# Two row products and a softmax sum ahead of a chain of small steps, and a move's wait split in two

## The chip, the cores and the metric

One Trainium2 chip, one core of it. The metric is the device time of one execution in microseconds (us), lower is better. Names of engines: PE is TensorE, DVE is VectorE, ACT is ScalarE, POOL is GpSimd, SP is SyncE. Each runs its own instructions in program order; between engines a semaphore wait decides.

## The reference

Four stages run one after the other on x of shape (16, 256, 128): a linear attention, a mixture of experts, a feature-map attention and a deep stage of six layers. Only the deep stage is touched. Its attention, for each of 16 sequences of 256 tokens and in each of six layers:

```python
qkv = x @ Wqkv                         # 128 -> 3 * 1024, 16 heads of 64
q = l2norm(q) * qs ; k = l2norm(k) * ksc
q = q * cos * scale + rotate_half(q) * sin * scale
k = k * cos * inv   + rotate_half(k) * sin * inv
sim = einsum(q, k over the own and the previous window of 32) * 8.0, masked
attn = softmax(sim, -1)
out = einsum(attn, v) ; x = out @ Wo + x
```

and then a feed-forward layer with a layer norm and an exact gelu, over blocks of two sequences. All in float32; the projections are split into a high and a low part.

## The kernel before, in words

The deep stage (`deep_stage`) is a software pipeline over 96 sequences (6 layers of 16), taken in pairs. A pair is a frame of 32 steps, 16 for its even and 16 for its odd sequence. In each step every engine runs, in this order: the late part of the attention of the sequence before, the early part of the attention of this one, the projection work of the sequence two ahead, the projection work of the sequence one ahead, and the feed-forward block's part. Tables of step numbers (`TOTAL_STEPS`, `NORM_STEPS`, `SCALE_STEPS`, `NEWTON_STEP` and others) say at which step a piece of work is issued; a step of 16 or more is one that falls into the next sequence's frame, and a negative one into that of the sequence two ahead or one ahead. The order on each engine is thus written out, and the engines wait for each other by semaphores.

Names and lines that matter here. For every sequence:

- DVE, L1900 `ss`: sums of squares of q and k per head, four reductions. L1919 to L1934, `inverse`: twelve dependent instructions on 128x64 numbers, the inverse square root by a bit trick and three Newton steps, result `rs`. They are issued at step 14 of a sequence for the sequence two ahead.
- DVE, L1906 and L1913: the rotary cosine product of a 128x1024 part of `raw`, and the addition of the sine part, which lies in `spare`. Four of each (k is the half of the tokens, part 0 is q, part 1 is k). Both read two tensors in SBUF.
- POOL, L2129: the sine products into `spare`, four. L2137: `raw` times `rs`, the scaling of q and k, four; the first of them is issued at step 14 and waits for `rs`. L2154: the softmax's product `E` times `rden`, two instructions of 128x512 for each group of eight heads.
- DVE, L1964 and L1970: row maximum of the scores and the subtraction, reading PSUM. ACT L1817: exp. DVE, L1977 and L1979, `totals`: row sum of `E` and its reciprocal `rden`.
- PE, L1654: transposes of `E`; L1565 to L1567: the projections, and the feed-forward's gate and up products; L1640: scores; L1672: attention times v.
- DVE, L2019 `xnT_lo`: low part of the feed-forward's input, at step 14 of the even sequence; PE's gate products (L1565) need it. L2027 `hT`: DVE's product of gate and up. L1941 and L1943 `xT_lo`: low part of the next projection's input. L2003 to L2012: the layer norm's statistics, in the frames' odd halves.
- SP, L1466 to L1469, `move_v`: sixteen DMAs that lay v out for the windows (`Vw`), after ACT has drained v's four parts from PSUM (L1801, `v_drained`). They are followed in SP's queue by the loads of `xs` and `xs4`.

The heads come in two groups of eight, o = 0 and o = 1. Group 1's sum, product and so on have the second number of each table.

Of the kernel before, what the change touches and what calls it, by code (L numbers as in the profile page):

```python
# [40 lines left out]
def count(n):  # L41


    return n + 1
# [1107 lines left out]
VS = 4  # L1152
# [19 lines left out]
SCORE_STEPS = (0, 5)  # L1172
HIGHEST_STEPS = (4, 10)
EXP_STEPS = (5, 12)
TOTAL_STEPS = (9, 15)
NORM_STEPS = (8, 16)
FLIP_STEPS = (11, 18)
MIX_STEPS = (13, 21)
DRAIN_STEPS = (15, 22)
# [108 lines left out]
def deep_stage(nc, X, c, w, kept, raw, split, wqkv_hi, wqkv_lo, out, x_out):  # L1288
    with ExitStack() as ctx:
# [5 lines left out]
        def sem(name):  # L1295
            counters.append(ctx.enter_context(nc.semaphore(name)))
            return counters[-1]
# [81 lines left out]
        v_drained = sem("v_drained")  # L1379
# [49 lines left out]
        def _(sp):  # L1429
# [28 lines left out]

            def move_v(n, par):

                sp.wait_ge(v_drained, count(VS * n + VS))
                for hp in range(2):
                    v = V[:, :, hp * 512:hp * 512 + 512]
                    own, back = 64 * hp + WIN, 64 * hp
                    for g in range(4):
                        sp.dma_start(Vw[own:own + WIN, par, :, g], v[g * WIN:g * WIN + WIN]).then_inc(v_moved[par], 16)  # L1466
                    for g in range(1, 4):
                        sp.dma_start(Vw[back:back + WIN, par, :, g], v[g * WIN - WIN:g * WIN]).then_inc(v_moved[par], 16)
                    sp.dma_start(Vw[back:back + WIN, par, 1, 0], v[P - WIN:P, 0]).then_inc(v_moved[par], 16)  # L1469
# [23 lines left out]
            def body(q):  # L1493
                if q.has(3):
                    bring(q, 3)
                if q.at(7) and q.has(2):
                    load_table(q.l + 1, 2)
                    load_table(q.l + 1, 3)
                if q.has(1):
                    move_v(q.n + 1, 1)  # L1500
                if q.opens(0) and q.has(0) and q.has(-1):
                    load_wo(q.l)
                if q.has_block(-1):
                    shift_block(q)
                if q.has(4):
                    bring(q, 4)
                if q.at(6) and q.has(4):
                    load_table(q.l + 1, 0)
                    load_table(q.l + 1, 1)
                if q.has(2):  # L1510
                    move_v(q.n + 2, 0)
# [6 lines left out]
            load_ffn(0)  # L1518
            bring(Pair(0, 0), 2)
            move_v(0, 0)  # L1520
            body(Pair(0, 0))
            body(Pair(0, 1))
# [370 lines left out]
        def _(dve):  # L1893
# [66 lines left out]
            def highest(n, o):  # L1960
                N = 2 * n + o
                dve.wait_ge(scored, count(N + 1))
                s = sco[:].rearrange("p b (c j) -> p (b c) j", j=HD)
                dve.tensor_reduce(mx[:], s, AX.X, ALU.max).then_inc(maxed, 1)  # L1964
                dve.wait_ge(maxed, count(N + 1))
                if not (isinstance(N, int) and N < 2):
                    dve.wait_ge(p_turned, count(2 * N - 2))
                s = sco[:].rearrange("p h (s j) -> p h s j", j=HD)
                m = mx[:].rearrange("p (h s) -> p h s", h=2)
                dve.tensor_tensor(E[:, o].rearrange("p (s h) j -> p h s j", h=2), s,  # L1970
                                  m[:, :, :, None].to_broadcast([P, 2, ROWS // 2, HD]),
                                  ALU.subtract).then_inc(lowered, 1)

            def totals(n, o):
                N = 2 * n + o
                dve.wait_ge(exped, count(N + 1))
                dve.tensor_reduce(den[:, o], E[:, o], AX.X, ALU.add).then_inc(totalled, 1)  # L1977
                dve.wait_ge(totalled, count(N + 1))
                dve.reciprocal(rden[:, o], den[:, o]).then_inc(recips, 1)  # L1979
# [7 lines left out]
            def attend(q, d, step):  # L1987

                for o in range(2):
                    if step == HIGHEST_STEPS[o]:  # L1990
                        highest(q.n + d, o)
                    if step == TOTAL_STEPS[o]:
                        totals(q.n + d, o)
# [123 lines left out]
        def _(pool):  # L2117
# [29 lines left out]
            def attend(n, step):  # L2147
                for o in range(2):
                    if step == NORM_STEPS[o]:
                        N = 2 * n + o  # L2150
# [196 lines left out]
```

## Time and profile before

| | |
|---|---|
| median of 3 runs | 4786.8 us (4783.35 to 4789.63) |
| the profiled execution | 4788.12 us, span 4786.4 us |
| DVE busy | 4071.3 us (85%) |
| PE busy | 4232.6 us (88%), matmul ends modelled |
| ACT busy | 3053.7 us (64%) |
| POOL busy | 3012.7 us (63%) |

The deep stage takes the stretch from about 1300 us to the end. It is periodic: a pair of sequences takes some 70 us. Busy time contains stretched time: an instruction that had to wait for something within itself is shown longer, not later. Idle time of an engine is shown ahead of the instruction that ended it, with the releaser.

### The profile page before, as it was taken

Reading aid. Unit: us, or ns where it says so; the run is one execution under the profiler, and the core shown is the slowest. Engines: PE = TensorE matmul, PEld = TensorE weight load, DVE = VectorE, ACT = ScalarE, POOL = GpSimd, SP = SyncE. Lnnn points to the kernel's source line nnn. Section 1 sums busy time; section 2 is a strip of 40 time slices with the busy share of each in tenths; the row PEclk is TensorE's granted clock in tenths of the full one; section 3 lists DMA queues with packets and bytes.
Section 4 is the critical chain, followed back from the end, with each engine's and each line's share of the span. In section 5 each row is a group of like instructions: output and inputs, shape, how many; then the busy total and the mean of one; then the engine's idle time right before and its main releaser. Section 6 shows DMA issues by size and latency. Waiting matters only on the chain.

```text
span 4786.4 us, 164817 instructions
## 1 busy us (share of the span) xinstructions
PE 4232.6 (88%) x70208; PEld 3350.3 (70%) x70208; DVE 4071.3 (85%) x6282; ACT 3053.7 (64%) x5515; POOL 3012.7 (63%) x1586
## 2 busy tenths in 40 slices
PE   5698699999668999999999998999989999999996
PEld 4566377877656777777777777777767777777775
DVE  4344699999788999999989999899998999989995
ACT  3365333333156777777777777777777777777773
POOL 0222566666267767677776777767776677766772
PEclk9699799999889999999999999999999999999998
DMA  1234000000023234232332323333242332433322
GB/s 50 78 127 141 0 1 0 0 0 0 19 54 76 58 70 95 63 81 62 75 88 64 84 58 90 80 67 75 60 101 66 67 77 58 96 74 67 75 58 74
DMA packets 237661, 302.78 MB, mean 63 GB/s; under 512 B 92500, under 2 KB 127832, under 8 KB 236504
## 3 DMA queue, kind: packets, MB, share of 16 engines
q1 hardware_dynamic: 221752, 247.08, 22.7%
q0 software_dynamic: 15264, 46.14, 3.1%
q8 instruction: 522, 8.55, 0.8%
q14 instruction: 123, 1.01, 0.1%
HBM read 50.37 MB, written 28.84 MB: 17 GB/s over the span
## 4 chain that ended last, share of the span: by engine, by line
DVE 41%; PE 14%; issue 9%; POOL 5%; ACT 4%; SPq 1%; DMA 0%; POOLq 0%; DVEq 0%; ACTq 0%
DVE raw L1906 10%; DVE raw L1913 8%; DVE mx L1964 3%; DVE E L1970 3%; DVE ss L1900 3%; PE shared L1565 2%; PE acc L1672 2%; DVE den L1977 2%; PE sco L1640 2%; POOL spare L2129 2%; POOL raw L2137 2%; DVE hT L2027 2%; PE shared L1567 2%; PE shared L1566 1%; ACT raw L1783 1%
## 5 line engine op out<-in xcount | busy, mean ns | idle before, releaser
L2137 POOL TENSOR_TENSOR raw<-raw,rs 128x1024 f32<-128x1024 f32 x384 | 794.4, 2069 | 887.4 <-DVE rs L1934 551.8
L2129 POOL TENSOR_TENSOR spare<-raw,table 128x1024 f32<-128x1024 f32 x384 | 969.7, 2536 | 79.1 <-DVE raw L1913 63.3
L1906 DVE TENSOR_TENSOR raw<-raw,table 128x1024 f32<-128x1024 f32 x384 | 667.9, 1739 | 87.1 <-POOL spare L2129 85.5
L1913 DVE TENSOR_TENSOR raw<-raw,spare 128x1024 f32<-128x1024 f32 x384 | 725.5, 1889 | 13.2
L1783 ACT ACTIVATE raw<-shared 128x512 f32<-128x512 f32 x768 | 463.2, 603 | 311.2 <-PE shared L1567 280.2
L1565 PE MATMUL shared<-wqkv_lo,xT_hi 128*128 128x512 f32 x1152 | 550.0, 477 | 57.1 <-DVE xT_lo L1943 49.0
L2154 POOL TENSOR_TENSOR E<-E,rden 128x512 f32<-128x512 f32 x384 | 544.2, 1438 | 30.8 <-DVE rden L1979 30.8
L1900 DVE TENSOR_REDUCE ss<-spare 128x16 f32<-128x1024 f32 x384 | 463.8, 1208 | 62.3 <-ACT spare L1788 61.9
L1620 PE MATMUL trn<-ident,raw 128*128 128x128 f32 x3072 | 485.2, 281 | 6.9 <-POOL raw L2137 3.4
L1567 PE MATMUL shared<-wqkv_hi,xT_hi 128*128 128x512 f32 x1152 | 462.6, 402 | 0.0
L1566 PE MATMUL shared<-wqkv_hi,xT_lo 128*128 128x512 f32 x1152 | 462.2, 401 | 0.0
L1788 ACT ACTIVATE spare<-shared 128x512 f32<-128x512 f32 x768 | 461.2, 601 | 1.3 <-DVE ss L1900 1.3
L1620 PEld LDWEIGHTS trn<-ident,raw 128*128 128x128 f32 x3072 | 352.6, 141 | 132.7 <-ACT qT L1810 76.5
L1672 PE MATMUL acc<-prT,Vw 64*64 64x32 f32 x24576 | 440.4, 221 | 2.2 <-issue 2.2
L1821 ACT ACTIVATE prT<-trn 128x512 f32<-128x512 f32 x384 | 232.0, 604 | 303.8 <-PE trn L1654 303.5
L1672 PEld LDWEIGHTS acc<-prT,Vw 64*64 64x64 f32 x24576 | 397.6, 136 | 25.3 <-issue 2.4
L1688 PE MATMUL shared<-wo,oT 128*128 128x128 f32 x3072 | 376.1, 276 | 2.3 <-ACT oT L1830 1.3
L1688 PEld LDWEIGHTS shared<-wo,oT 128*128 128x128 f32 x3072 | 363.4, 193 | 8.6 <-ACT spare L1788 1.5
L1640 PE MATMUL sco<-kT,qT 64*32 64x64 f32 (+1 forms) x24576 | 354.8, 223 | 12.5 <-issue 12.2
L1640 PEld LDWEIGHTS sco<-kT,qT 64*32 64x32 f32 x24576 | 240.9, 108 | 169.7 <-issue 165.4
L1654 PE MATMUL trn<-ident,E 128*128 128x128 f32 x1536 | 250.1, 287 | 112.9 <-POOL E L2154 109.1
L1565 PEld LDWEIGHTS shared<-wqkv_lo,xT_hi 128*128 128x128 f32 x1152 | 221.7, 192 | 133.7 <-issue 43.0
(208 smaller groups left out, 9678.4 us busy)
## 6 DMA issues: line engine op xcount, KB each, us to landing
Vw<-V SPq DMA_DIRECT2D x1344, 128.0 KB
xs<-X SPq DMA_DIRECT2D x144, 128.0 KB, 2.6
Vw<-V SPq DMA_DIRECT2D x192, 64.0 KB
e_plain<-in_L_ffn_W SPq DMA_DIRECT2D x16, 704.0 KB, 4.6
split_hi<-e_high POOLq DMA_DIRECT2D x16, 704.0 KB, 5.9
split_lo<-e_low POOLq DMA_DIRECT2D x16, 704.0 KB, 7.0
wqkv_hi<-split_hi POOLq DMA_DIRECT2D x30, 256.0 KB, 3.1
wqkv_lo<-split_lo POOLq DMA_DIRECT2D x30, 256.0 KB, 3.2
```

The lines of the kernel that those rows point to most:

```text
L1565: pe.matmul(to, a_hi, b_lo, start=True, stop=False)
L1567: return pe.matmul(to, a_hi, b_hi, start=False, stop=True)
L1620: t = pe.transpose(trn[:, r * P:(r + 1) * P], raw[:, par, k, part, at:at + P], c["ident"][:])
L1640: t = pe.matmul(sco[g * WIN:g * WIN + WIN, hp, at:at + back + WIN], qT[lo:lo + 64, r, at_q:at_q + WIN], kT[lo:lo + 64, r, at_q - back:at_q ...
L1672: t = pe.matmul(acc[hp][64 * jp:64 * jp + 64, at:at + WIN], Vw[lo:lo + 64, par, k, g, (4 * o + j) * HD:(4 * o + j + 1) * HD], prT[lo:lo + ...
L1688: t = pe.matmul(to[:, k * P:(k + 1) * P], oT[:, r, k * P:(k + 1) * P], wo[:, r], start=(r == 0), stop=(r == PAIRS - 1))
L1900: dve.tensor_reduce(ss[:, j * H:(j + 1) * H], heads_of(sq[:, part]), AX.X, ALU.add).then_inc(reduced, 1)
L1906: dve.tensor_tensor(x, x, table[:, part, 0, k][:, None, :].to_broadcast([P, H, HD]), ALU.mult).then_inc(cos_part, 1)
L1913: dve.tensor_tensor(x, x, t2[:, part], ALU.add).then_inc(summed, 1)
L2129: pool.tensor_tensor(dst, src, by[:, None].to_broadcast([P, H, 2, 32]), ALU.mult).then_inc(sin_part, 1)
L2137: pool.tensor_tensor(x, x, rs[:, at:at + H][:, :, None].to_broadcast([P, H, HD]), ALU.mult).then_inc(rotated, 1)
L2154: pool.tensor_tensor(E[:, o, rows], E[:, o, rows], rden[:, o, rows][:, :, None].to_broadcast([P, ROWS // 2, HD]), ALU.mult).then_inc(norme ...
```

## The change

Three edits, all in the deep stage.

1. DVE's `totals` for the second eight heads moves from step 15 to step 14. Within step 14 the attention part comes first, so it now stands ahead of the twelve instructions of `inverse`.
2. POOL's product `E` times `rden` for the second eight heads moves from step 16 to step 14. It now stands ahead of the first scaling of q.
3. `move_v` waited once for all four parts of v; now it waits for two parts ahead of its first eight DMAs, and for all four ahead of its second eight.

```diff
-TOTAL_STEPS = (9, 15)
-NORM_STEPS = (8, 16)
+TOTAL_STEPS = (9, 14)
+NORM_STEPS = (8, 14)
...
             def move_v(n, par):
 
-                sp.wait_ge(v_drained, count(VS * n + VS))
                 for hp in range(2):
+                    sp.wait_ge(v_drained, count(VS * n + 2 * hp + 2))
                     v = V[:, :, hp * 512:hp * 512 + 512]
```

On DVE, around the end of an odd sequence, before the change (`na` and `rs` are Newton's, `den` and `rden` the sum and its reciprocal, `xT_lo` the next projection's input):

```order
 L1931 SCALAR_TENSOR_TENSOR na<-na,rs 128x64
 L1934 SCALAR_TENSOR_TENSOR rs<-na,rs 128x64
 L1977 TENSOR_REDUCE den<-E 128x16
 L1979 RECIPROCAL rden<-den 128x16
 L1941 TENSOR_TENSOR xT_lo<-shared,xT_hi 64x256
```

and the same place after it, from the last reduction of the squares:

```order
 L1900 TENSOR_REDUCE ss<-spare 128x16
 L1977 TENSOR_REDUCE den<-E 128x16
 L1979 RECIPROCAL rden<-den 128x16
 L1919 TENSOR_SCALAR hx<-ss 128x64
 L1921 TENSOR_SCALAR na<-hx 128x64
 L1925 TENSOR_TENSOR rs<-magic,na 128x64
```

The sum and the reciprocal moved from behind the twelve instructions to before them.

On DVE at the end of an even sequence, where the feed-forward's `xnT_lo` and `hT` stand, before:

```order
 L1934 SCALAR_TENSOR_TENSOR rs<-na,rs 128x64
 L2019 TENSOR_TENSOR xnT_lo<-hT,xnT_hi 128x512
 L1977 TENSOR_REDUCE den<-E 128x16
 L1979 RECIPROCAL rden<-den 128x16
 L1941 TENSOR_TENSOR xT_lo<-shared,xT_hi 64x256
 L1943 TENSOR_TENSOR xT_lo<-shared,xT_hi 64x256
 L2027 SCALAR_TENSOR_TENSOR hT<-shared,b,hT 128x512
```

and after:

```order
 L1934 SCALAR_TENSOR_TENSOR rs<-na,rs 128x64
 L2019 TENSOR_TENSOR xnT_lo<-hT,xnT_hi 128x512
 L1941 TENSOR_TENSOR xT_lo<-shared,xT_hi 64x256
 L1943 TENSOR_TENSOR xT_lo<-shared,xT_hi 64x256
 L2027 SCALAR_TENSOR_TENSOR hT<-shared,b,hT 128x512
```

Between `xnT_lo` and `hT` the sum and the reciprocal are gone.

On POOL, one sequence, before (the first `raw` row is the first scaling of q, `E` the second eight heads' product, `spare` the sine products):

```order
 L2129 TENSOR_TENSOR spare<-raw,table 128x1024
 L2137 TENSOR_TENSOR raw<-raw,rs 128x1024
 L2154 TENSOR_TENSOR E<-E,rden 128x512 x2
 L2137 TENSOR_TENSOR raw<-raw,rs 128x1024 x2
 L2129 TENSOR_TENSOR spare<-raw,table 128x1024
```

and after:

```order
 L2129 TENSOR_TENSOR spare<-raw,table 128x1024
 L2154 TENSOR_TENSOR E<-E,rden 128x512 x2
 L2137 TENSOR_TENSOR raw<-raw,rs 128x1024 x3
 L2129 TENSOR_TENSOR spare<-raw,table 128x1024
```

The two instructions on `E` moved ahead of the first scaling, and the three scalings now follow one another.

## Rows read from the trace of the kernel before

**Rows 1.** Busy time by engine in a stretch (us, PE, PEld, DVE, ACT, POOL, clock, DMA)
```profile
2000.00:3000.00 1000.00, 921.79 (x18923) 730.60 (x18923) 932.49 (x1230) 759.77 (x1328) 729.72 (x383) 0.99 0.34 75
```
**Rows 2.** Part 4 of the page, the chain that ended last, by engine
```profile
DVE 41%; PE 14%; issue 9%; POOL 5%; ACT 4%; SPq 1%; DMA 0%; POOLq 0%; DVEq 0%; ACTq 0%
```
**Rows 3.** Groups by line, DVE, 1400 to 4700 us (busy us, mean ns, idle)
```profile
L1913 DVE TENSOR_TENSOR raw<-raw,spare 128x1024 f32<-128x1024 f32 x374 | 703.2, 1880 | 12.8
L1906 DVE TENSOR_TENSOR raw<-raw,table 128x1024 f32<-128x1024 f32 x374 | 650.2, 1739 | 80.8 <-POOL spare L2129 79.3
```
**Rows 4.** Timeline of DVE, end of an even sequence (start us, us)
```profile
2240.86 0.19 DVE L1919 TENSOR_SCALAR hx<-ss 128x64 f32<-128x64 f32 x1
2241.09 0.20 DVE L1921 TENSOR_SCALAR na<-hx 128x64 int32<-128x64 int32 x1
...
2243.66 0.22 DVE L1934 SCALAR_TENSOR_TENSOR rs<-na,rs 128x64 f32<-128x64 f32 x1
2243.80 0.68 DVE L2019 TENSOR_TENSOR xnT_lo<-hT,xnT_hi 128x512 fp32r<-128x512 f32 x1
2244.40 1.21 DVE L1977 TENSOR_REDUCE den<-E 128x16 f32<-128x1024 f32 x1
2245.65 0.25 DVE L1979 RECIPROCAL rden<-den 128x16 f32<-128x16 f32 x1
2245.82 0.35 DVE L1941 TENSOR_TENSOR xT_lo<-shared,xT_hi 64x256 fp32r<-64x256 f32 x1
...
2246.65 0.75 DVE L2027 SCALAR_TENSOR_TENSOR hT<-shared,b,hT 128x512 f32<-128x512 f32 x1
2247.32 2.02 DVE L1906 TENSOR_TENSOR raw<-raw,table 128x1024 f32<-128x1024 f32 x1
2249.36 2.81 DVE L1913 TENSOR_TENSOR raw<-raw,spare 128x1024 f32<-128x1024 f32 x1
2252.10 1.21 DVE L1964 TENSOR_REDUCE mx<-sco 128x16 f32<-128x1024 f32 x1
```
**Rows 5.** Timeline of POOL, an odd and an even sequence's end
```profile
2211.41 2.04 POOL L2154 TENSOR_TENSOR E<-E,rden 128x512 f32<-128x512 f32 x2
2213.41 1.91 POOL L2137 TENSOR_TENSOR raw<-raw,rs 128x1024 f32<-128x1024 f32 x1
2215.27 1.99 POOL L2184 TENSOR_TENSOR small<-small,halves 128x4 f32<-128x4 f32 x1
...
2243.96 2.29 POOL L2137 TENSOR_TENSOR raw<-raw,rs 128x1024 f32<-128x1024 f32 x1 [5.35 <-DVE rs L1934]
2246.21 2.04 POOL L2154 TENSOR_TENSOR E<-E,rden 128x512 f32<-128x512 f32 x2
2248.21 2.88 POOL L2137 TENSOR_TENSOR raw<-raw,rs 128x1024 f32<-128x1024 f32 x1
```
**Rows 6.** Timeline of DVE, end of an odd sequence
```profile
2206.45 0.20 DVE L1919 TENSOR_SCALAR hx<-ss 128x64 f32<-128x64 f32 x1
...
2209.24 0.23 DVE L1934 SCALAR_TENSOR_TENSOR rs<-na,rs 128x64 f32<-128x64 f32 x1
...
2212.76 0.72 DVE L2012 TENSOR_SCALAR small<-mv 128x4 f32<-128x4 f32 x1
...
2214.28 2.12 DVE L1906 TENSOR_TENSOR raw<-raw,table 128x1024 f32<-128x1024 f32 x1
...
2217.69 1.23 DVE L1964 TENSOR_REDUCE mx<-sco 128x16 f32<-128x1024 f32 x1
```
**Rows 7.** Timeline of DVE, late, the same L2012 with POOL idle
```profile
4757.30 0.17 DVE L2012 TENSOR_SCALAR small<-mv 128x4 f32<-128x4 f32 x1
```
**Rows 8.** Waits, 1000 to 4700 us (us in total, times, longest)
```profile
POOL raw L2137 <- DVE rs L1934: 551.8, 96, 6.6
PE trn L1654 <- POOL E L2154: 109.1, 91, 4.1
DVE mx L1964 <- PE sco L1640: 16.4, 7, 3.8
```
**Rows 9.** Timeline of ACT, the exp ahead of the odd sum
```profile
2204.63 1.06 ACT L1817 ACTIVATE E<-E 128x1024 f32<-128x1024 f32 x1
```
**Rows 10.** Waits of SP's own queue, 1500 to 4650 us
```profile
SPq L1466 <- ACT V L1801: 1756.4, 90, 27.5
```

## The prediction, made before the changed kernel ran

> **What bounds the kernel.** I read the busy times by stretch first. In the deep stage PE and DVE are both busy over 92% of the time, ACT and POOL some 75% [rows 1]. The chain that ended last is mostly DVE, 41% of the whole span against PE's 14% [rows 2]. The reader should then look at how long DVE's two largest groups take. L1906 and L1913 average 1.74 and 1.88 us [rows 3], though the sum over a 128x1024 tile takes 1.21 us [rows 4], and single ones of these two take 1.2 us when POOL does nothing. So a good part of "busy" DVE is waiting inside its instructions.
>
> The timelines of DVE and POOL side by side show for what. L1906 starts at 2247.32, lasts 2.02 and ends at 2249.34; POOL's two products on E end at 2248.25 [rows 4, 5], about 1.1 us before that. POOL's next scaling, started at 2248.21, takes 2.88 us instead of 1.91, and L1913 behind L1906 takes 2.81 and ends at 2252.17, 1.1 us after that scaling. The two engines take turns, one instruction at a time: whoever comes second waits for the whole instruction of the other. It is no matter of size: the layer norm's 4-element L2012 takes 0.72 us beside POOL's product on E and ends with it (2213.48 against 2213.45) [rows 5, 6], and 0.17 us with POOL idle [rows 7]. Sums over a tile (L1977, L1964) stay at 1.21 to 1.23 us whatever POOL does.
>
> That row decides this case, because the twelve Newton instructions now run alone. POOL is idle through them in every one of the 96 sequences, waiting for their result [rows 8], so each takes 0.19 to 0.23 us and they follow at 0.26 us: 2240.86 to 2243.88, 3.02 us [rows 4]. The change starts the two E products just when they begin.
>
> **The change part by part.** Time 0 below is where Newton starts before. I follow the DVE until it starts the maximum of the next scores (L1964), which before is at 11.24 in the even sequence (2252.10) and at 11.24 in the odd one (2217.69) [rows 4, 6]. From there the engines' order is as before.
>
> *The sum and its reciprocal ahead.* Work is only exchanged: 1.42 us (2244.40 to 2245.82) [rows 4] go before Newton instead of behind. Newton starts at 1.42, and without any disturbance ends at 4.44.
>
> *E ahead of the first scaling.* The reciprocal ends at 1.50; POOL starts what it waited for 0.08 us after its releaser (2243.88 to 2243.96), so at 1.58. Each of the two products takes 1.02 us [rows 5]. Newton's first instruction is through by then. The second is ready at 1.65 and waits for the first product, to 2.6: 0.95 lost. It takes a turn, the second product follows (2.7 to 3.7), and the third instruction waits 0.85. Behind that POOL has nothing that could run, the scaling needs `rs`. So Newton is stretched by 1.8 us and ends at 6.25 instead of 3.02. The trace has no Newton instruction beside POOL; the bounds of this term are 0 (if instructions this small are not held, as those that sum are not) and 2.06 (both products whole). I take 1.8, by the L2012 row, which is as small and is held.
>
> The Trainium skill ("SBUF — State Buffer", section "SBUF: two separate sides") says that VectorE and GpSimd share a pair of ports as an exclusive lock, taken by VectorE instructions with two SBUF inputs or in a two-port mode, and that "the other fully blocks". It speaks against this change, as ten of the twelve have two SBUF inputs. By that rule the stretch is the 1.8 us taken here; the trace agrees with 0.72 against 0.17 us.
>
> *Even sequence, behind Newton.* POOL: first scaling from 6.33; beside `xnT_lo` it takes 2.25 to the next start, the second scaling 1.86, so POOL is occupied to 10.44 [rows 5]. DVE: `xnT_lo` 0.60. Then PE's gate products, gelu and `hT`: before, `hT` started 2.17 us after `xnT_lo` ended (2244.48 to 2246.65), and the sum and `xT_lo` covered that exactly. The sum's 1.42 are gone from there, only `xT_lo`'s 0.8 is left, so DVE now idles up to 1.35 us and starts `hT` at about 9.0. After its 0.67 L1906 is asked for at 9.7, in the middle of the second scaling, and waits to 10.44 (this wait would be there without the idle time too, so the idle time costs nothing of its own here). L1906 1.21 and L1913 1.23, which now meets no POOL instruction, bring L1964 to 12.85: 1.6 us later. What was gained is inside: L1906 and L1913 were held 2.4 us together, now 0.75.
>
> *Odd sequence.* POOL's two scalings follow from 6.33 at 1.86 each, to 10.1. DVE reached L1906 4.81 us behind Newton (2209.47 to 2214.28) [rows 6]; take off 1.42 for the sum and 0.5 for L2012, which meets the change of two scalings and waits little: asked at 9.15, held to 10.1. With L1906 and L1913 L1964 starts at 12.55, 1.3 us later. POOL's power instruction (1.99, L2184) falls beside L1913 as before and does not hold it.
>
> *What PE gets.* E is ready some 3 us earlier, and PE's wait for it, 109.1 us in 91 cases [rows 8], mostly goes. But DVE waited for scores only 7 times, 16.4 us in all [rows 8]: PE stood ahead of DVE at that place, so this is worth at most 16 us. And in the even sequence PE gets `xnT_lo` 3.2 us later, its gates end 3.2 us later, so its own wait for E is replaced by that one.
>
> *The moves of v.* The first eight DMAs start two drains earlier. SP's queue is idle 1756.4 us over 90 such waits [rows 10], nobody is shown waiting for `Vw` or for room in V. Behind the new second wait stand eight DMAs and the loads of `xs`, `xs4`, which go out no later than before since the count is the same. I cost it at 0; if the cover of some 20 us per sequence were gone it would show as a PE wait.
>
> **The sum.** (1.6 + 1.3) / 2 = 1.45 us over 96 sequences: 139 us. Chunk-loading frames and the 16 us of PE are of either sign and are left inside the range. The profiled execution took 4788.1 us, so 4927; the median of the runs lies 1.3 below it: 4926. The delay sits on the chain of waits, as DVE is on it without a gap from the second eight heads' maximum through Newton to L1964 of the next sequence, and the PE and ACT work behind starts from L1970.
>
> **Rivals.**
> - *Newton is not held* (faster). Ends at 4.44; L1906 starts when the scalings end, at 8.63 and 8.24, and L1964 at 11.05 and 10.7: 0.2 and 0.55 us earlier, 36 us in all, 4751. For it: no row shows a 64-element two-input instruction held, and the reductions aren't. Against: L2012. It decides at a stretch of 0.35 us: below that the change gains.
> - *Held once.* The two products run without a gap and Newton's second and third share one wait, or POOL starts late. Stretch 0.95, L1964 at 12.0 and 11.7: 0.6 us per sequence, 4844. Against: after each of its products POOL let DVE in (L1906 was let in between E and the scaling).
> - *A new wait decides as well.* The exp of the second heads ends at 2205.69 [rows 9], 0.76 us before Newton begins in the odd sequence; the sum now stands right there and Newton no longer covers it. Where ACT is late this adds up to 0.5 us per odd sequence, and PE, 2 us late in the even one, some 0.35 more: 41 us on top, 4967.
> - *Nothing moves the end*, PE being the bound and DVE's extra hidden: within 10 us of 4787. Against: L1964 waits for PE seven times in 96.
>
> **Chances.** Forecast 0.67, held once 0.12, new wait as well 0.06, not held 0.11, nothing 0.04. A time can be told from no change by about 0.2%, 10 us. So slower 0.85, same 0.04, faster 0.11. The range, 4825 to 4970, holds the forecast, the one with the new wait and most of held once; it leaves out the not-held case.
>
> **What would show it.** Right: the second and third Newton instruction (L1921, L1925, or one of the next) at about 1 us each, sum of L1919 to L1934 up by some 170 us over 96 sequences; L1906 and L1913 down by some 100 us; POOL's wait for `rs` still there, shorter by E's 2.1 but longer by the stretch; DVE idle ahead of `hT` up to 1.35 us in even sequences; PE's wait for E nearly gone, its wait for `xnT_lo` longer; no wait on `Vw`. Wrong: Newton's instructions still at 0.2 us with POOL's E products beside them.

## The result, and the profile after

The changed kernel takes 4925.8 us (median of 4 runs, 4922.16 to 4931.44), the kernel before beside it 4788.2: a ratio of 1.029, 95% interval 1.0277 to 1.0303. The change costs 138 us. The forecast was 4926; its total is right, and its working is right in part only.

Part 1 of the page after: DVE has lost busy share, not gained it.

```profile
PE 4297.2 (87%) x70208; PEld 3418.1 (69%) x70208; DVE 4049.1 (82%) x6282; ACT 3050.5 (62%) x5515; POOL 2862.8 (58%) x1586
```

The chain that ended last, which was DVE 41% and PE 14% [rows 2]:

```profile
PE 46%; DVE 15%; issue 7%; ACT 4%; POOL 1%; DMA 0%; POOLq 0%; DVEq 0%; SPq 0%
```

The groups of DVE by line, 1400 to 4800 us (busy us, mean ns | idle), against [rows 3] and the two lines of the kernel before that follow:

```profile
L1906 DVE TENSOR_TENSOR raw<-raw,table 128x1024 f32<-128x1024 f32 x371 | 646.8, 1743 | 62.4 <-POOL spare L2129 60.5
L1913 DVE TENSOR_TENSOR raw<-raw,spare 128x1024 f32<-128x1024 f32 x371 | 540.5, 1457 | 12.7
L1900 DVE TENSOR_REDUCE ss<-spare 128x16 f32<-128x1024 f32 x372 | 451.5, 1214 | 128.4 <-ACT spare L1788 128.4
...
L1929 DVE TENSOR_TENSOR na<-rs,hx 128x64 f32<-128x64 f32 x279 | 132.1, 473 | 9.6
L1925 DVE TENSOR_TENSOR rs<-magic,na 128x64 int32<-128x64 int32 x93 | 86.0, 925 | 5.4 <-DVE na L1921 2.6
```

```profile
L1900 DVE TENSOR_REDUCE ss<-spare 128x16 f32<-128x1024 f32 x373 | 450.6, 1208 | 56.7 <-ACT spare L1788 56.3
...
L2027 DVE SCALAR_TENSOR_TENSOR hT<-shared,b,hT 128x512 f32<-128x512 f32 x144 | 107.1, 744 | 17.8 <-ACT hT L1859 10.9 <-PE shared L1567 5.7
```

Two of Newton's twelve are held: L1925 takes 0.925 us, and L1929, which comes three times per sequence, averages 0.473. Against 0.225 each that is 0.70 + 3 x 0.25 = 1.44 us per sequence. L1913 meets fewer of POOL's instructions, 1.46 us instead of 1.88; L1906 is as before.

So the hold as such does not show up in DVE's busy time. It is 139 us over the 96 sequences, and L1913 gives back 159. What grows is DVE's idle time: ahead of `hT` from 17.8 to 95.2 us, and ahead of the sums of squares (L1900), which wait for ACT, from 56.7 to 128.4. The loss appears as waits for PE and ACT.

The end of one even sequence on DVE and on POOL (start us, us), to be read beside [rows 4, 5]:

```profile
2202.28 1.21 DVE L1900 TENSOR_REDUCE ss<-spare 128x16 f32<-128x1024 f32 x1
2203.41 1.21 DVE L1977 TENSOR_REDUCE den<-E 128x16 f32<-128x1024 f32 x1
...
2204.99 0.20 DVE L1921 TENSOR_SCALAR na<-hx 128x64 int32<-128x64 int32 x1
2205.22 0.95 DVE L1925 TENSOR_TENSOR rs<-magic,na 128x64 int32<-128x64 int32 x1
2206.20 0.97 DVE L1929 TENSOR_TENSOR na<-rs,hx 128x64 f32<-128x64 f32 x1
...
2209.16 0.69 DVE L2019 TENSOR_TENSOR xnT_lo<-hT,xnT_hi 128x512 fp32r<-128x512 f32 x1
...
2212.95 0.75 DVE L2027 SCALAR_TENSOR_TENSOR hT<-shared,b,hT 128x512 f32<-128x512 f32 x1 [2.33 <-PE shared L1567]
2213.62 1.22 DVE L1906 TENSOR_TENSOR raw<-raw,table 128x1024 f32<-128x1024 f32 x1
...
2216.62 1.23 DVE L1964 TENSOR_REDUCE mx<-sco 128x16 f32<-128x1024 f32 x1 [0.53 <-PE sco L1640]
```

```profile
2204.98 2.10 POOL L2154 TENSOR_TENSOR E<-E,rden 128x512 f32<-128x512 f32 x2 [4.96 <-DVE rden L1979]
2209.32 4.14 POOL L2137 TENSOR_TENSOR raw<-raw,rs 128x1024 f32<-128x1024 f32 x2 [2.24 <-DVE rs L1934]
```

POOL's two products run 2204.98 to 2207.08, and the two held instructions end with the first of them and with the second (2206.17, 2207.17). Newton's 3.02 us became 4.42 (2204.82 to about 2209.24). Then the part that the forecast priced at nothing: DVE idles 2.33 us ahead of `hT`. PE had waited since the end of its transposes for `xnT_lo`, and when it starts, its granted clock is the lower one. PE's timeline and the granted clock of the stretch:

```profile
2209.95 0.77 PE L1565 MATMUL shared<-xnT_lo,w_hi 128*128 128x512 f32 x1 [3.87 <-issue]
2210.51 0.63 PE L1566 MATMUL shared<-xnT_hi,w_lo 128*128 128x512 f32 x1
```

```profile
2209.90:2213.00 3.10, 3.05 (x8) 2.40 (x9) 0.75 (x3) 0.69 (x1) 3.10 (x2) 0.50 0.73 163
2213.00:2216.00 3.00, 3.00 (x43) 2.10 (x41) 2.97 (x3) 0.87 (x2) 0.47 (x1) 0.61 0.41 87
2216.00:2222.00 6.00, 6.00 (x150) 4.54 (x149) 5.10 (x6) 5.83 (x11) 4.26 (x2) 1.00 0.08 25
```

The column before the last two is the clock: 0.50, the lower of TensorE's two levels (1.2 GHz), behind an idle time of 3.87 us, and back at 1.00 after some 6 us. The products start 0.43 us apart instead of 0.23.

The waits after, 1000 to 4850 us (us in total, times, longest):

```profile
POOL raw L2137 <- DVE rs L1934: 221.2, 96, 5.3
PE shared L1565 <- issue: 191.0, 50, 4.4
...
PE shared L1565 <- DVE xT_lo L1943: 114.6, 46, 12.3
DVE hT L2027 <- PE shared L1567: 95.2, 45, 2.3
...
DVE mx L1964 <- PE sco L1640: 19.5, 25, 3.2
DVE den L1977 <- ACT E L1817: 18.1, 32, 3.0
```

The first two waits of PE in the kernel before, in the same stretch:

```profile
PE shared L1565 <- issue: 60.6, 50, 1.7
...
PE shared L1565 <- DVE xT_lo L1943: 49.0, 37, 12.3
```

PE's wait for E (109.1 us) [rows 8] is down to 4.2 us in 3 cases, and two others grew: the one ahead of the gates, whose input is `xnT_lo`, from 60.6 to 191.0 us, and the one for `xT_lo` from 49.0 to 114.6. In the odd sequence the sum now waits for its exp in some cases, 18.1 us in 32. PE never waits for `Vw`.

### The profile page after: what moved, and what is told of

Read it like the earlier page. It is cut to its first block, busy times and chain, and to the rows that moved or that the text cites. A ratio compares the mean times of both kernels' runs of the same rounds, so it can differ in the third digit from the quotient of the medians.

```text
span 4929.8 us, 164817 instructions
## 1 busy us (share of the span) xinstructions
PE 4297.2 (87%) x70208; PEld 3418.1 (69%) x70208; DVE 4049.1 (82%) x6282; ACT 3050.5 (62%) x5515; POOL 2862.8 (58%) x1586
## 4 chain that ended last, share of the span: by engine, by line
PE 46%; DVE 15%; issue 7%; ACT 4%; POOL 1%; DMA 0%; POOLq 0%; DVEq 0%; SPq 0%
PE shared L1565 8%; PE shared L1567 6%; PE acc L1672 6%; PE shared L1566 6%; PE shared L1688 6%; PE trn L1620 6%; PE sco L1640 5%; DVE raw L1906 3%; PE trn L1654 3%; PE sco L1630 2%; DVE na L1929 1%; DVE den L1977 1%; DVE E L1970 1%; DVE mx L1964 1%; DVE raw L1913 1%
## 5 line engine op out<-in xcount | busy, mean ns | idle before, releaser
L2137 POOL TENSOR_TENSOR raw<-raw,rs 128x1024 f32<-128x1024 f32 x384 | 750.4, 1963 | 646.5 <-DVE raw L1913 425.2
L2129 POOL TENSOR_TENSOR spare<-raw,table 128x1024 f32<-128x1024 f32 x384 | 938.6, 2455 | 166.9 <-DVE raw L1913 142.8
L2154 POOL TENSOR_TENSOR E<-E,rden 128x512 f32<-128x512 f32 x384 | 468.2, 1239 | 475.6 <-DVE rden L1979 475.6
L1906 DVE TENSOR_TENSOR raw<-raw,table 128x1024 f32<-128x1024 f32 x384 | 669.6, 1744 | 70.7 <-POOL spare L2129 68.7
L1565 PE MATMUL shared<-wqkv_lo,xT_hi 128*128 128x512 f32 x1152 | 562.2, 488 | 140.7 <-DVE xT_lo L1943 114.6
L1913 DVE TENSOR_TENSOR raw<-raw,spare 128x1024 f32<-128x1024 f32 x384 | 566.4, 1475 | 13.2
L1900 DVE TENSOR_REDUCE ss<-spare 128x16 f32<-128x1024 f32 x384 | 465.9, 1213 | 134.1 <-ACT spare L1788 134.1
L1565 PE MATMUL shared<-xnT_lo,w_hi 128*128 128x512 f32 (+1 forms) x288 | 143.4, 498 | 182.9 <-issue 171.1
```

The source lines that it names most:

```text
L1565: pe.matmul(to, a_hi, b_lo, start=True, stop=False)
L1906: dve.tensor_tensor(x, x, table[:, part, 0, k][:, None, :].to_broadcast([P, H, HD]), ALU.mult).then_inc(cos_part, 1)
L1913: dve.tensor_tensor(x, x, t2[:, part], ALU.add).then_inc(summed, 1)
L2129: pool.tensor_tensor(dst, src, by[:, None].to_broadcast([P, H, 2, 32]), ALU.mult).then_inc(sin_part, 1)
L2137: pool.tensor_tensor(x, x, rs[:, at:at + H][:, :, None].to_broadcast([P, H, HD]), ALU.mult).then_inc(rotated, 1)
L2154: pool.tensor_tensor(E[:, o, rows], E[:, o, rows], rden[:, o, rows][:, :, None].to_broadcast([P, ROWS // 2, HD]), ALU.mult).then_inc(norme ...
```

## The experiments

Theory H says that POOL's products hold Newton and that this is the loss. Theory O says that the order itself costs: what waits for `rs`, `xnT_lo` and `xT_lo` comes 1.42 us later. Theory P says that PE's wait and its slower clock are a part of it. Ratios are to the kernel before on the same chip.

### One edit at a time

```diff
# e1_sum_only, from the kernel before
-TOTAL_STEPS = (9, 15)
+TOTAL_STEPS = (9, 14)
# e2_product_only, from the kernel before
-NORM_STEPS = (8, 16)
+NORM_STEPS = (8, 14)
# e3_moves_only: the third edit of the change alone
```

> Only DVE's sum ahead of Newton; POOL's product stays behind the first scaling. Theory H (what costs is that POOL's products on E hold Newton, 1.44 us per sequence in the changed kernel's trace): Newton's twelve run at 0.2 us again, and if nothing else counted the kernel would be near before, 4790. Rival O (what costs is the order itself: everything that waits for rs and for xnT_lo comes 1.42 us later on an engine that has no other work to put there): L1906 and L1913 meet E and the second scaling as before, only 1.4 to 1.9 us later, so about 4920 to 4950, with Newton unheld. The two differ by some 130 us.

> Only POOL's product on E ahead of the first scaling, the sum stays behind Newton. Newton is not held under any theory (POOL is idle until the sum's reciprocal). H: near before, 4790. O: the three scalings start 2 us later than before and the last sine product with them, DVE's wait for it grows from 0.9 to up to 2.8 us, of which part is hidden: 4830 to 4900.

> Only v's moves in two parts. All theories: within 0.2% of before, SP issues its first eight DMAs some 5 us earlier and nobody waits for them; over 10 us either way would say that the DMAs' place matters.

Measured: the sum alone 4949.0 (1.0325, 1.0308 to 1.0342), the product alone 4932.3 (1.0297, 1.0281 to 1.0313), the moves alone 4783.9 (0.9988, 0.9979 to 0.9997). The moves are within 0.2% of before, 5 us faster by the medians. Each of the other two alone costs as much as the whole change, though Newton isn't held in either (L1929 mean 225 ns in both). H as the only cause falls. O has the direction of both; the sum alone lies in its range, the product alone above its 4830 to 4900.

With the sum alone, POOL's E comes behind a first scaling that itself starts later, and PE waits for it; DVE waits for the last sine product. Waits of that kernel, 1400 to 4800 us:

```profile
PE trn L1654 <- POOL E L2154: 149.2, 102, 5.8
...
DVE raw L1906 <- POOL spare L2129: 122.7, 86, 3.2
```

With the product alone the scalings come behind the sum and E. PE's wait for E falls from 105.7 to 77.1 us, but DVE's wait for the sine product grows from 79.3 [rows 3] to 173.7 us:

```profile
DVE raw L1906 <- POOL spare L2129: 173.7, 92, 3.3
```

So the two moves belong together. The costs don't add up: 160 us for one, 144 for the other, 138 for all three. Neither is the harmful one of a pair; each repairs a part of what the other breaks.

### What the late input of the gates costs

```diff
# e4_after_low13, from the changed kernel
-B_LOW_STEP = 14
+B_LOW_STEP = 13
# e7_after_pe_filled, from the changed kernel, PE ahead of a block's first gate
# (the waits for the bank and for w1 moved up, ahead of these lines)
+                        for _ in range(12):
+                            pe.matmul(bank_of("f_gate", t, 0)[0:rows, :], w1_hi[:, FH + lo:FH + lo + rows],
+                                      xnT_hi[:], start=True, stop=True)
+                        pe.wait_ge(f_low, count(m + 1))
```

> The changed kernel with the feed-forward's xnT_lo one step earlier on DVE, ahead of the sum and of Newton, so that PE's gate products do not wait 3.9 us and DVE's hT does not wait 2.3 us; Newton is held as in the changed kernel. H: the hold is most of the loss, the even sequence gains about 0.5 us, 24 us in all, so about 4900. Theory P (in the even sequence the late xnT_lo lets PE fall idle, its granted clock falls to half for the gate products and the chain of waits goes over PE): 1.5 to 2.5 us per pair come back, 4810 to 4850, PE's granted clock back at 0.99 in the deep stage, and the chain goes back to DVE.

> The changed kernel with twelve more products of 128x512 on PE ahead of the gates of each block (their result is overwritten), in the time in which PE would wait for xnT_lo; DVE, POOL and ACT as in the changed kernel. P: if the fall of the clock is what makes the gates 0.43 instead of 0.23 us, they run at 0.23 again, DVE's wait ahead of hT falls from 2.3 to about 1.2 us and 20 to 50 us come back: 4880 to 4905. If the clock is no part of the loss: 4925.

Measured: 4881.4 (1.0191, 1.0176 to 1.0207) and 4886.9 (1.0207, 1.0192 to 1.0223). They bring back 45 and 41 of the 138 us, each measured from the kernel before beside it. The first is more than H's 24 and less than P's range (4810 to 4850) asked for; the second lies in P's range. Both put the chain back on DVE. Of the kernel with the filled PE:

```profile
DVE 46%; PE 12%; issue 7%; ACT 4%; POOL 4%; DMA 0%; DVEq 0%; POOLq 0%; SPq 0%
```

```profile
L1932 DVE TENSOR_TENSOR na<-rs,hx 128x64 f32<-128x64 f32 x282 | 133.4, 473 | 9.7
...
L2030 DVE SCALAR_TENSOR_TENSOR hT<-shared,b,hT 128x512 f32<-128x512 f32 x92 | 68.8, 748 | 55.7 <-ACT hT L1862 55.7
```

And two of its gate products, 0.23 us apart:

```profile
2198.40 0.39 PE L1566 MATMUL shared<-xnT_hi,w_lo 128*128 128x512 f32 x1
2198.63 0.39 PE L1567 MATMUL shared<-xnT_hi,w_hi 128*128 128x512 f32 x1
```

Its lines stand three further down, L1932 is L1929 and L2030 is L2027. Newton is held as in the changed kernel (473 ns), `hT` waits 55.7 us instead of 95.2, and the only edit is more work for PE. So the wait was lengthened by the clock, and about 40 us of the loss are that.

The first of the two gains in another way. Its mean clock stays at 0.96 (2000 to 3000 us), where 0.99 was expected and where the changed kernel stands too; PE now waits for `xT_lo` instead (231.3 us in 88). DVE's idle time ahead of `hT` goes from 95.2 to 4.1 us, yet L1906 and L1913 together take 1333 us instead of 1187, as they meet POOL's scalings again. Most of that idle time had only stood where a hold would have stood.

### The product with and without its length

```diff
# e8_after_short_product, from the changed kernel; e9_before_short_product, from the kernel before
+                            if o == 1:
+                                rows = slice(jj * (ROWS // 2), jj * (ROWS // 2) + 1)
...
```

> The changed kernel with the second eight heads' product on POOL cut to a sixteenth (64 of 512 numbers per instruction, the rest of that normalisation is left out), so that it holds Newton for a tenth of the time and the order stays. H: Newton ends 1.3 us earlier, so up to 96 times 1.3 = 125 us come back: about 4800. O and P: only part, as xnT_lo and rs are still 1.42 us later than before: PE still waits 2.5 us or more in the even sequence: 4830 to 4870.

> The kernel before with the second eight heads' product cut to a sixteenth (the rest of that normalisation is left out), as control for e8_after_short_product: what is the product worth in its old place, between the first and the second scaling, where it meets L1906 and L1913. If the place beside Newton is what makes it dear (H), it is worth much less here than the 164 us there: the timeline of before has these two held 0.7 to 2.3 us by E or by the scaling behind it, of which the scalings would take up most, so 10 to 70 us: 4720 to 4780. If the product costs the same in both places, about 4630.

Measured: 4761.4 (0.9939, 0.9924 to 0.9954) and 4715.2 (0.9845, 0.9829 to 0.9862). Each instruction of the product works on 64 of 512 numbers, which is an eighth and not the sixteenth of the expectations, and takes 0.32 and 0.31 us instead of 1.02. The rest of that normalisation is left out.

The product's length is worth 4925.8 - 4761.4 = 164 us in the new place and 4789.8 - 4715.2 = 75 us in the old one. The second lies just outside what H expected (10 to 70). The first is more than H's 125, and far more than O and P allowed. With the product cut, the change still costs 4761.4 - 4715.2 = 46 us, and that kernel's chain is PE's (48%). The 138 us thus split into 90 that depend on where the product stands and 46 that don't.

Where the product's length goes can be read from DVE's groups, 1400 to 4800 us. The new place, product cut:

```profile
L1906 DVE TENSOR_TENSOR raw<-raw,table 128x1024 f32<-128x1024 f32 x374 | 658.9, 1762 | 73.4 <-POOL spare L2129 71.7
L1913 DVE TENSOR_TENSOR raw<-raw,spare 128x1024 f32<-128x1024 f32 x374 | 575.5, 1539 | 12.9
L1900 DVE TENSOR_REDUCE ss<-spare 128x16 f32<-128x1024 f32 x373 | 452.4, 1213 | 83.8 <-ACT spare L1788 83.5
...
L1929 DVE TENSOR_TENSOR na<-rs,hx 128x64 f32<-128x64 f32 x282 | 63.6, 226 | 9.7
```

The old place, product cut:

```profile
L1906 DVE TENSOR_TENSOR raw<-raw,table 128x1024 f32<-128x1024 f32 x374 | 695.7, 1860 | 72.6 <-POOL spare L2129 71.0
L1913 DVE TENSOR_TENSOR raw<-raw,spare 128x1024 f32<-128x1024 f32 x374 | 575.0, 1537 | 12.8
```

In the new place Newton's hold goes (473 to 226 ns for L1929), and with it 45 us of idle time ahead of the sums of squares; L1906 and L1913 get no shorter, but 0.02 and 0.08 us longer. In the old place Newton was never held; there L1913 falls from 1.88 to 1.54 us while L1906 rises from 1.74 to 1.86, some 83 us less for the two together, and no other group moves as much. So what the new place adds is Newton's hold and what comes behind it. Whether the 46 us that are left are the same as the 40 of PE's clock was not tested: no run has both the short product and a filled PE.

### Earlier still

```diff
# e10_sum_at_13, from the changed kernel
-TOTAL_STEPS = (9, 14)
+TOTAL_STEPS = (9, 13)
# e11_sum_at_13_exp_11: also
-EXP_STEPS = (5, 12)
+EXP_STEPS = (5, 11)
-B_LOW_STEP = 14
+B_LOW_STEP = 13
# e12_before_exp_11: the kernel before with EXP_STEPS = (5, 11) alone
```

> The changed kernel with the sum one step earlier, ahead of the last reduction of squares too. POOL's two products then run beside that reduction (1.2 us, not held) and only their last 0.85 us meets Newton. H: the hold falls from 1.44 to about 0.5 us per sequence, so 90 us would come back, less what DVE now waits for the exp in odd sequences (it is 1.2 us earlier there and had 0 to 0.7 to spare; up to 1.2 x 48 = 58 us): 4870 to 4900. O and P alone (the hold costs nothing, only lateness does): nothing comes back, 4925 to 4980.

> As e10_sum_at_13, with the exp of the second heads one step earlier on ACT and xnT_lo at step 13 on DVE (behind the reduction, ahead of Newton). If hold, PE's wait with its slower clock, and the exp are all that the change costs, this is the sum of their removals: 44 us of e4_after_low13, some 90 of the hold and the exp's wait: 4790 to 4830. If rs being 1.42 us later than before is a cost of its own, it stays at 4840 to 4870.

> The kernel before with only the exp of the second heads one step earlier on ACT. It is the control of e11_sum_at_13_exp_11: the sum is issued 3 us behind the reductions here and does not wait for the exp, so nothing is won by it; ACT's moves of v and of the first probabilities come 1.06 us later (2.3 with the table load in odd sequences), which PE's mix may wait for: 4785 to 4830.

Measured: 4936.0 (1.0302, 1.0285 to 1.0319), 4817.3 (1.0057, 1.0039 to 1.0075) and 4808.8 (1.0041, 1.0027 to 1.0056). The first missed H's range (4870 to 4900) and lies in that of O and P alone (4925 to 4980); the second and third lie in the ranges given. Groups of DVE in the first:

```profile
L1977 DVE TENSOR_REDUCE den<-E 128x16 f32<-128x1024 f32 x185 | 224.1, 1212 | 56.2 <-ACT E L1817 56.2
L1919 DVE TENSOR_SCALAR hx<-ss 128x64 f32<-128x64 f32 x93 | 98.7, 1061 | 3.2
```

The hold fell from 1.44 to 1.061 - 0.195 = 0.87 us, less than I had worked out, since the reduction covers only the first product and the second holds Newton's first instruction; and the sum now waits 56.2 us for the exp instead of 15 to 18. What one gave, 55 us, the other and PE, on which the chain still lies (49%), took. The hold was thus cut without a gain, which H alone can't explain.

The second kernel takes away the wait for the exp and PE's wait ahead of the gates as well (168.6 us to 21.1) and comes to within 8.5 us of its control, the third; both lie below the changed kernel and above the one before. Nearly all of the change's cost can so be undone, but no gain is left: the exp's new place costs 19 us on its own. Newton is still held there, L1919 with a mean of 1.047 us against 0.195, some 80 us over the 96 sequences. A hold of that size is therefore not a loss of that size by itself; it depends on what stands behind it.

### Two on the kernel before and on the sum

```diff
# e5_moves_low13: e3_moves_only with B_LOW_STEP = 13
# e6_sum_low13: e1_sum_only with B_LOW_STEP = 13
```

> The kernel before with v's moves in two parts and xnT_lo one step earlier (ahead of Newton). P (PE's gates wait for xnT_lo even before, 1.2 to 1.7 us in even sequences): PE gets it 3 us earlier; as the chain of before lies on DVE and not on these gates, only the first scaling's start loses its 0.39 us beside xnT_lo: 0 to 20 us faster than before. O: Newton and rs come 0.6 us later in the even sequence, 48 times 0.6 = 29 us slower at most.

> The sum alone ahead of Newton, with xnT_lo ahead of both; Newton not held. Against e1_sum_only (4949): P says PE's wait and the fall of its clock were a good part of that, and 40 to 60 us come back, as in e4_after_low13: about 4900. O says the lateness of rs is the rest and stays: POOL's scalings 1.42 us later on both sequences with E still between them, so not below 4890. If all of the sum's cost were PE's it would be 4790.

Measured: 4792.3 (1.0006, 0.9997 to 1.0015) and 5025.7 (1.0491, 1.0475 to 1.0507). The first shows no gain, against P, and stays within O's bound of a loss of at most 29 us. The second is far outside every range: `xnT_lo` ahead of the sum makes that kernel 77 us slower, where with the product moved too it made it 45 us faster. Waits of the second:

```profile
PE trn L1654 <- POOL E L2154: 309.4, 110, 5.8
...
DVE mx L1964 <- PE sco L1640: 151.6, 47, 3.8
```

PE runs the gates early and then stands before E, which POOL finishes later still; the scores behind E are late for DVE. Why the wait doubles from 149.2 us, where DVE's instructions only changed places by 0.6 us, I can't say from this; it was not followed further.

## Why the prediction was right, and where it was not

- **Newton held**: right in kind, too large in size. 1.8 us was taken, 1.44 measured. The second instruction slips through (0.20 us), the third and fourth are held (the forecast had the second and third), and each loses 0.7 to 0.75 us instead of 0.95 and 0.85. "Not held" and "held once" are out: POOL and DVE took turns, as forecast. The Trainium skill ("SBUF — State Buffer", section "SBUF: two separate sides") gives the shared pair of ports, in the cases that it names, to whichever engine starts first, for its whole instruction. The trace agrees for two-input instructions of 64 elements (0.95 and 0.97 against 0.225 us). `TENSOR_SCALAR`, with one input, is held as well in the kernel with the sum at 13 (1.061 against 0.195); the rule has that for a two-port mode, and the trace does not show in which mode it ran.
- **"The idle time costs nothing of its own" in the even sequence**: right for DVE's next instruction, wrong for PE. The forecast took gates at their old speed; PE idled 3.87 us, its clock fell to 0.50, and `hT` started 3.1 us after `xnT_lo` ended instead of 2.17. With PE filled, DVE reaches L1906 1.0 us earlier in the even sequences, but POOL then holds it longer, and it ends only 0.1 us earlier (means over the trace). What the slow PE does cost comes elsewhere: in the even sequence L1964, which needs PE's scores, follows 0.25 us later, and in the odd one the sum starts 0.38 us later, behind its exp. The chain ran over PE, and about 40 us of the 138 are there, by the run with PE filled.
- **The stretch that was followed**: from Newton's old start to L1964 the means over the trace are 12.7 us in even and 12.8 in odd sequences, forecast 12.85 and 12.55, before 11.4 and 11.3. That is 1.4 us more per sequence, forecast 1.45; outside this stretch 0.1 us is added.
- **"Work is only exchanged"**: the exchange of 1.42 us is no exchange for the others. The sum alone costs 160 us with Newton unheld. In the sum of the forecast this was contained because both sequences were followed to L1964 instead of adding up parts.
- **The exp's cover gone**: a rival's half, named and real, but small: 18.1 us in 32 cases. It needs the late PE too: from 1400 us on the wait is 15.2 us, with PE filled 3.7, and 5.1 in the kernel before.
- **PE's gain from an early E**: its wait of 109.1 us went, as forecast, and other waits took its place, as forecast; no gain from it shows.
- **POOL's wait for `rs`**: forecast a little shorter (2.1 less, 1.8 more), measured 551.8 to 221.2 us, 3.4 less per sequence. The wait moved ahead of the product, where POOL now waits 453.5 us for `rden`; the time is not lower but split.
- **L1906 and L1913**: down by 159 us for L1913 (725.5 to 566.4, whole execution) and by nothing for L1906 (667.9 to 669.6), forecast some 100 for both.
- **v's moves**: 0 taken; -0.12%, which is inside the 0.2% that the forecast called nothing, though the interval (-0.21 to -0.03%) lies just below no change.

Errors of opposite sign cancelled: 0.36 us too much per sequence for the hold (35 us if it counted in full), some 40 us too little for PE. The closeness of 4926 to 4925.8 is luck to that extent; with one error alone the forecast would have been near 4890 or 4965 (an estimate from these two terms). The mechanism and the size of the stretch were right.

## What to carry to other kernels

Before moving a POOL product, list what DVE runs in the new place by what it reads: here sums and instructions with a PSUM input were not held (1.21 and 1.22 us throughout), a chain of small dependent SBUF instructions was, one of them for each POOL instruction, until that one ended, however small the held one was. Then ask what stands behind the hold, since part of it may be paid back there. Ask of every short instruction sequence that moves ahead of a shared result who waits for the instruction behind it (here `xnT_lo`), and count for PE not only the wait but the slower products behind it. And where two moves are made together, price each alone too: here each alone was worse than, or as bad as, both.

## What was not expected of the hardware

A PE that idled 3.87 us ran its next six products of 128x512 0.43 us apart, at a granted clock of 0.50 (1.2 GHz), and was back at 1.00 some 6 us later; giving it twelve useless products in that time made the kernel 39 us faster. In the kernel before, with an idle time of 1.21 us in the same place, the clock stayed at 1.00:

```profile
2244.59 0.47 PE L1565 MATMUL shared<-xnT_lo,w_hi 128*128 128x512 f32 x1 [1.21 <-issue]
```

```profile
2244.50:2247.30 2.80, 1.63 (x6) 1.05 (x7) 2.72 (x5) 1.67 (x2) 2.80 (x3) 1.00 0.93 202
```
